# New orders in the attention of a ViT block, and a bias row added to h by GpSimd

## The reference

```
h = tokens(x)                                   # 5 shifted copies, layer norm over 3840 features, @ w (3840 x 192) + b
h = h + attention(layernorm(h))                 # 12 heads of 16, out @ out_w.T + out_b
h = h + experts(layernorm(h))                   # 8 experts, the two largest of a softmax, gelu(x @ w1 + b1) @ w2 + b2
```

## Time and profile before

| | |
|---|---|
| median of 3 runs | 201.43 us (200.71 to 201.55) |
| the profiled execution, its own time | 201.66 us |
| its span, first to last instruction | 199.9 us |
| PE busy | 178.9 us (89%) |
| DVE busy | 142.8 us (71%) |
| ACT busy | 115.4 us (58%) |
| POOL busy | 77.6 us (39%) |
| TensorE on the chain that ended last | 69% of the span |
| granted TensorE clock, mean | 0.983 |

### The profile page before, as it was taken

The page is one execution under the profiler, slowest core; times in us unless marked ns, Lnnn a source line. Parts: engine busy times, 40 slices in busy tenths (PEclk is TensorE's granted clock), DMA queues, the critical chain, the costliest instruction groups (busy, mean ns, idle before and its releaser), DMA issues.

```text
span 199.9 us, 3458 instructions
## 1 busy us (share of the span) xinstructions
PE 178.9 (89%) x1136; PEld 154.3 (77%) x1136; DVE 142.8 (71%) x319; ACT 115.4 (58%) x206; POOL 77.6 (39%) x102
## 2 busy tenths in 40 slices
PE   0599999985798987698999999999999999999994
PEld 0489749954566845577899999989989999989894
DVE  5487994498908638449976976878869869778753
ACT  2485753741221428456569579677596696785540
POOL 7873001125805051187034546266245344462000
PEclk9999999999859999999999999999999999999999
DMA  6999999100010177002700280450630810000002
GB/s 123 223 303 298 260 225 227 29 0 2 0 39 3 31 260 183 3 0 69 208 3 0 65 210 0 135 141 2 183 93 2 239 34 2 0 3 0 0 0 79
DMA packets 14691, 18.38 MB, mean 92 GB/s; under 512 B 2435, under 2 KB 10744, under 8 KB 14678
## 3 DMA queue, kind: packets, MB, share of 16 engines
q1 hardware_dynamic: 14134, 18.19, 34.3%
q10 hardware_dynamic: 544, 0.03, 0.2%
HBM read 17.44 MB, written 0.39 MB: 89 GB/s over the span
## 4 chain that ended last, share of the span: by engine, by line
PE 69%; DVE 11%; issue 6%; DMA 5%; ACT 3%; POOL 2%; SPq 2%; DVEq 0%; POOLq 0%; ACTq 0%
PE ps L371 30%; PE ps L1140 16%; PE ps L1142 7%; DMA early<-in_x 4%; DVE big_r L1215 3%; PE ps L826 2%; PE ps L1002 2%; PE ps L1184 1%; PE ps L1183 1%; DVE merge L1286 1%; PE ps L1182 1%; DVE norm L1393 1%; PE ps L939 1%; PE ps L828 1%; DMA shifted<-shifted 1%
## 5 line engine op out<-in xcount | busy, mean ns | idle before, releaser
L371 PE MATMUL ps<-big_r,wsplit 128*128 128x512 f32 (+1 forms) x255 | 62.8, 383 | 0.0
L1140 PE MATMUL ps<-wsplit,big_r 128*128 128x384 f32 x168 | 49.7, 355 | 0.7 <-DVE big_r L1215 0.7
L751 ACT ACTIVATE early<-ps,b1t 128x512 f32<-128x512 f32 x48 | 32.8, 683 | 29.8 <-PE ps L371 29.8
L1215 DVE TENSOR_TENSOR big_r<-early,big_r 128x512 fp32r<-128x512 f32 x48 | 38.4, 802 | 16.1 <-ACT big_r L333 15.6
L371 PEld LDWEIGHTS ps<-big_r,wsplit 128*128 128x128 f32 x255 | 43.1, 188 | 6.4
L1142 PE MATMUL ps<-wsplit,big_r 128*128 128x192 f32 x168 | 42.1, 250 | 0.0
L1140 PEld LDWEIGHTS ps<-wsplit,big_r 128*128 128x128 f32 x168 | 31.5, 188 | 3.0 <-DVE big_r L1215 0.9
L1142 PEld LDWEIGHTS ps<-wsplit,big_r 128*128 128x128 f32 x168 | 32.0, 190 | 1.3
L333 ACT ACTIVATE big_r<-early 128x512 fp32r<-128x512 f32 x48 | 30.3, 632 | 1.5
L1550 DVE SCALAR_TENSOR_TENSOR merge<-sq,gates,merge 128x192 f32<-128x192 f32 x32 | 26.9, 864 | 0.0
L1574 DVE SCALAR_TENSOR_TENSOR t_a<-ps,gates,merge 128x192 f32<-128x192 f32 x28 | 10.3, 412 | 6.3 <-PE ps L1142 6.3
(11 more groups left out here) (227 smaller groups left out, 290.3 us busy)
## 6 DMA issues: line engine op xcount, KB each, us to landing
stage<-in_L_ffn_w SPq DMA_DIRECT2D x4, 576.0 KB, 6.1
early<-in_L_ffn_w SPq DMA_DIRECT2D x4, 576.0 KB, 5.8
shifted<-in_L_tok_w SPq DMA_DIRECT2D x6, 288.0 KB, 9.6
early<-in_x SPq DMA_DIRECT2D x3, 512.0 KB, 7.0
stage<-in_L_ffn_w SPq DMA_DIRECT2D x4, 384.0 KB, 4.0
stage<-in_L_ffn_w SPq DMA_DIRECT2D x8, 192.0 KB, 4.9
early<-in_L_ffn_w SPq DMA_DIRECT2D x4, 384.0 KB, 3.2
early<-in_L_ffn_w SPq DMA_DIRECT2D x8, 192.0 KB, 3.8
```

The lines of the kernel that those rows point to most:

```text
L371: mm = nc.tensor.matmul(dst, lhs, rhs, start=(first and n == 0), stop=(last and n == 4))
L751: nc.scalar.activation(gf[:, j % NG], ps[:, HPB[j % 4], :], ACT.Gelu, bias=b1t[:, bass.ds(k, 1)]).then_inc(s_gelu, 1)
L1140: nc.tensor.matmul(ps[:, AB[t], 0:2 * D], g_hi[:, j % NG, tok], w2c, start=(f == 0), stop=False)
L1215: return nc.vector.tensor_tensor(o, a, b, op)
```

## The change

It touches four engines' lists.

- GpSimd waits for both low parts of `n1` (`s_nlo` at 2) before it begins the low parts of expert 0.
- GpSimd then adds `const_row` to all of `h` in place (128 x 768 elements), waiting for `s_n` (all of `n1` written, so `h` is no longer read by the norm) and for `s_row`. `constant_rows` and its two TensorE products are gone; `projection` starts the bank itself; `residual` waits for the new semaphore `s_hrow`.
- TensorE makes `values(2)` and `values(3)` right behind `transposed_k(1)`; `repeated_v(0)` and `repeated_v(1)` move behind `near_by_heads(1)`.
- ScalarE copies the values of group 1 before `near_rows(1)`; the four `split_high(1, ...)` of expert 1 are spread over the attention: two behind `values(0)`, one behind `transposed_p(0)`, one behind `exponentials(1)`. None is left behind the gelu table.

```diff
--- before.py
+++ after.py
@@ -236,8 +236,8 @@
         s_ptps, s_pt, s_pv, s_nvp, s_nv, s_pvn, s_ao, s_aodup = (
             sem(n) for n in ("s_ptps", "s_pt", "s_pv", "s_nvp", "s_nv", "s_pvn", "s_ao", "s_aodup"))
 
-        s_vbias, s_row, s_at, s_ahi, s_alo, s_op, s_h2 = (
-            sem(n) for n in ("s_vbias", "s_row", "s_at", "s_ahi", "s_alo", "s_op", "s_h2"))
+        s_vbias, s_row, s_hrow, s_at, s_ahi, s_alo, s_op, s_h2 = (
+            sem(n) for n in ("s_vbias", "s_row", "s_hrow", "s_at", "s_ahi", "s_alo", "s_op", "s_h2"))
 
         s_n2t, s_n2hi, s_n2lo = (sem(n) for n in ("s_n2t", "s_n2hi", "s_n2lo"))
         s_rl, s_rlsb, s_rt, s_gsub, s_gexp, s_gtop, s_gidx, s_gate = (
@@ -550,8 +550,14 @@
                 if g == 0:
                     rstd(0, 0)
             rstd(0, 1)
+            pool.wait_ge(s_nlo, G)
             split_low_w1(pool, 0, 0)
             split_low_w2(pool, 0, 0)
+
+            pool.wait_ge(s_n, TT)
+            pool.wait_ge(s_row, 1)
+            nc.gpsimd.tensor_tensor(h[:, :, :], h[:, :, :], const_row[:, :].unsqueeze(1).broadcast_to([P, TT, D]),
+                                    ALU.add).then_inc(s_hrow, 1)
 
             def near_values(g):
 
@@ -720,26 +726,26 @@
             last_columns_again(0, 1, n1)
             high_parts(1, s_nt, NTB, nt, s_nhi)
             values(0)
+            act.wait_ge(s_emb, G)
+            act.wait_ge(d_stage[1], 16 * STAGE_DMAS)
+            split_high(1, 0)
+            split_high(1, 1)
             near_rows(0)
             transposed_q(1)
             exponentials(0)
+            values(1)
             near_rows(1)
             transposed_p(0)
-            values(1)
+            split_high(1, 2)
             exponentials(1)
+            split_high(1, 3)
             transposed_p(1)
-            act.wait_ge(s_emb, G)
-            act.wait_ge(d_stage[1], 16 * STAGE_DMAS)
-            split_high(1, 0)
             for g in range(G):
 
                 act.wait_ge(s_ao, g + 1)
                 copy(ao[:, 2 * g:2 * g + 2, D:], ao[:, 2 * g:2 * g + 2, P:D]).then_inc(s_aodup, 1)
                 high_parts(g, s_at, ATB, aot, s_ahi)
             nc.scalar.activation(table_in[:], neg_half[:, 0:1], ACT.Gelu)
-            split_high(1, 1)
-            split_high(1, 2)
-            split_high(1, 3)
             for g in range(G):
                 last_columns_again(1, g, n2)
                 high_parts(g, s_n2t, N2B, n2t, s_n2hi)
@@ -1035,12 +1041,6 @@
                                           ptsb[:, b * S:(b + 1) * S], vbd[0:PROWS, b], start=True, stop=True)
                 mm.then_inc(s_pv, 1)
 
-            def constant_rows(g):
-
-                pe.wait_ge(s_pt, g + 1)
-                nc.tensor.matmul(ps[:, OB[g], 0:2 * D], ones_f[0:1, :],
-                                 const_row[0:1, :].unsqueeze(1).broadcast_to([1, 2, D]), start=True, stop=False)
-
             def projection(g):
 
                 pe.wait_ge(s_ahi, g + 1)
@@ -1048,7 +1048,7 @@
                 for n in range(2):
                     tok = slice((2 * g + n) * P, (2 * g + n + 1) * P)
                     mm = triple(ps[:, OB[g], n * D:(n + 1) * D], lambda a: aot[:, a, tok],
-                                wx_(slice(OUT0, OUT0 + D)), True, first=False, last=(n == 1))
+                                wx_(slice(OUT0, OUT0 + D)), True)
                 mm.then_inc(s_op, 1)
 
             pe.wait_ge(s_meansq, 1)
@@ -1089,22 +1089,20 @@
             transposed_q(1)
             near_scores(0)
             transposed_k(1)
+            values(2)
+            values(3)
+            strided_scores(1)
+            near_by_heads(1)
             repeated_v(0)
             repeated_v(1)
-            strided_scores(1)
-            near_by_heads(1)
             transposed_p(0)
-            values(2)
-            values(3)
             near_scores(1)
             strided_values(0)
             repeated_v(2)
             repeated_v(3)
             transposed_p(1)
-            constant_rows(0)
             transposes(0, ao, s_ao, lambda t: t // 2 + 1, ATB, s_at, s_aodup)
             strided_values(1)
-            constant_rows(1)
             projection(0)
             pe.wait_ge(s_vbd, TT)
             transposes(1, ao, s_ao, lambda t: t // 2 + 1, ATB, s_at, s_aodup)
@@ -1498,6 +1496,7 @@
             def residual(g):
 
                 dve.wait_ge(s_op, g + 1)
+                dve.wait_ge(s_hrow, 1)
                 ts = slice(2 * g, 2 * g + 2)
                 tt(h2[:, ts], h[:, ts], ps[:, OB[g], 0:2 * D].rearrange("p (t n) -> p t n", t=2),
                    ALU.add).then_inc(s_h2, 1)
```

## The result

| | before | after |
|---|---|---|
| median of 4 runs | 201.49 us (200.71 to 205.25) | 192.54 us (192.19 to 195.73) |
| ratio, with its 95% interval | | 0.9562 (0.9524 to 0.9601) |
| profiled execution, its own time | 201.66 us | 192.19 us |
| its span | 199.9 us | 190.5 us |
| PE, DVE, ACT, POOL busy | 178.9, 142.8, 115.4, 77.6 us | 170.2, 140.1, 115.6, 80.4 us |

The change makes the kernel faster by 9 us. The ratio leaves out the slowest run of each kernel (205.25 and 195.73 us), which lies over 1.5% above that kernel's fastest.

A forecast was written before the change was run, and what follows sets the result against it. TensorE was taken as the bound, with 69% of the chain, and gains arising between 38 and 82 us: 3.06 + 2.82 + 1.38 - 0.57 + 0.6 = 7.3, less 0.3, so 201.43 - 7.0 = 194.4 us; range 193.2 to 197.4.

The forecast's parts named there:

- values sooner: Second half of the attention: group 1's values made before `repeated_v`, so `outputs(1)` gains 1.38 us more than the maximum.
- Collision of the normalisations: First norm, group 1: with GpSimd waiting for `s_nlo`, VectorE's two normalisations fall from 3.73 to 0.67, gaining 3.06 us.
- Clock: TensorE after the gap at 48.28 to 51.75 us: without the gap the clock stays full, gaining 2.82 us.
- The clock falls all the same: Rival, chance 0.16: TensorE's clock still falls, early or in a remaining shorter gap; price 2.8, giving 197.2 us.
- One of the shorter gaps: Within the clock rival: TensorE's remaining waits at 66.5, 70.0 or 74 us, where the clock might fall; price 2.8.
- Addition: GpSimd before `near_values(0)`: adding 768 columns takes 2.0 us (bounds 1.80 and 2.64), so `outputs(0)` waits 0.2.
- costs nothing either way: `outputs(0)` and `near_values(1)` holding each other cost 0, since ScalarE's duplicate of `ao(0)` waits for `transposed_p(1)` until 64.8.
- Given back: From `outputs(1)` to `projection(1)`: `projection(0)` no longer lies inside the wait for GpSimd, losing 0.57 us.
- Splits: Second norm: ScalarE's splits no longer delay the duplicates of `n2`, gaining 0.6 us; their new places are covered.
- I take 0.3 off for semaphore steps: Deduction of 0.3 us from the summed gain for semaphore steps on the six changed links, leaving 7.0.
- GpSimd as the bound: Rival, chance 0.15: slower addition or blocked denominators put 0.6 to 1.5 us into the chain at 61 to 63 us.
- GpSimd blocking everything: Rival, chance 0.02: GpSimd blocks every VectorE instruction, those from PSUM too, costing 8.4 us and giving 202.8 us.

The follow-up runs named there:

- e9: The change with the addition to `h` moved between `near_values(0)` and `near_values(1)` on GpSimd: 192.6 us.
- e7: The change with the constant rows made by TensorE again and no addition to `h` on GpSimd: 193.52 us.
- e14: The kernel before plus GpSimd's wait for `s_nlo` and the new order of values and `repeated_v`; constant rows and splits as before: 193.83 us.
- e6: The change with the four `split_high(1, ...)` of expert 1 back in their old places on ScalarE: 193.17 us.
- last version: The change with the addition between the near values and GpSimd's power of the gates ahead of expert 1's `w2` low parts, without warm products: 191.62 us.

## Why the forecast was right, and where it failed

The mechanisms were right: collision, clock and late DMA went as forecast. What failed are sizes in the sum. The gain up to the router was put at 7.3 and then 7.0; it was 7.99. The term that failed most is *values sooner*, put at 1.38 by a walk that was too long, and measured at 1.72: 0.34. The first maximum adds 0.16, the stretch behind `outputs(1)` 0.19, and 0.3 was taken off without a row. With all that set right the forecast would be 193.4, still inside the range; what puts the median below it are another 0.9 us, for which the prediction has no term.

- *Collision of the normalisations, 3.06.* Right: 0.67 after, 3.73 without the wait and 3.80 with the gap filled. GpSimd's low parts are where they were put, 50.07 + 1.45 = 51.52 on the clock of before against 51.5.
- *Clock, 2.82.* Right, with its cause: 2.89 with the gap filled and nothing else (2.77 against the second profile of before). "The clock falls all the same" came true in three partial kernels but not in the change. "One of the shorter gaps" fits only one of them: the kernel with the old order of the values, where the fall comes 1.0 us behind a gap of 2.00. With the wait alone (66.5 us) and with the gap filled (68.8) TensorE had no gap over 0.2 us in the 2 us before it. I had not foreseen that the order of the values also guards against that fall; it is worth 1.6 us beside its own 1.74.
- *Values sooner, 1.38.* Right in kind; 1.72 measured. Here lies the step that failed first, the walk along TensorE's list: "`transposed_p(0)` to 60.95, `near_scores(1)` to 61.5" came at 59.66 + 1.45 = 61.11, and the duplicate of `ao(0)`, forecast for 64.8, at 64.33. I added whole durations of groups, but neighbours in the timeline overlap by 0.1 to 0.2 us, so each joint added a little. In the row of `outputs(1)` the sum of it is 0.50.
- *Addition, 2.0.* It took 1.80, the lower bound, the subtraction of the same size. Read from both sizes, 2 x 1.00 - 1.80 = 0.20 of the 1.00 does not grow with the columns (an estimate), and my scaling counted it twice. `outputs(0)` waited 0.24 for it, as forecast (0.2), but that GpSimd's lateness there "costs nothing either way" was wrong: the duplicate of `ao(0)` started 0.04 behind VectorE's held product (61.78 + 1.06 = 62.84), and TensorE waited 0.53 for that product. It cost some 0.18, which the addition between the near values gives back (e9). The edit as a whole was worth 0.21 where I had counted 0 (e7). That it speaks against the engine split of the Trainium skill, "GPSIMD Engine Reference", § 4.1 Engine selection, did little harm here: moving it off the place ahead of `near_values(0)` brought 0.18 in N to R and nothing in the time.
- *Given back, -0.57.* Measured -0.49.
- *Splits, 0.6.* The total of 0.81 is near, but 0.55 of it is the one part that stood ahead of the duplicate of `ao(0)`; the prediction passed over it there and put all 0.6 at the second norm, where 0.26 was due. In the sum the 0.55 is part of the 1.72: with the splits in their old places that term is 1.18 (e14). The walk already had them moved, so its 1.38 held this part without naming it. The 0.26 and the 0.49 given back are not apart either: from `outputs(1)` to the router it takes 8.19 before, 8.22 in e6 and 7.96 in the change, so what is given back at `projection(1)` is regained by the router in any case.
- *"I take 0.3 off for semaphore steps".* Wrong. No row stood behind it; the steps were already in the walk, which was too long and not too short.
- *Rivals.* No reduction or reciprocal was held: the reduction `den` of group 1 started at 63.70, while the addition that GpSimd began at 63.65 ran, and took 0.39 as alone. GpSimd as the bound came about in kind (it stands on the chain up to `outputs(0)`), at 0.18 instead of 0.6 to 1.5. GpSimd blocking everything did not come about; nothing was given back in the experts (117.55 and 117.59).

The whole error: 0.69 in the walk (0.16 at the first maximum, 0.34 to `outputs(1)`, the rest behind it), 0.3 taken off, and 0.9 by which the medians differ more (8.9) than N to R (8.0). The last is no effect that I could tie to an edit. The first stage, whose code is the same, differed by 1.45 us in the two profiled executions; and runs of the kernel before have mean clocks from 0.991 (span 197.1) to 0.949, so some run longer at the lower clock than its profile shows and some less, while the change has none below 0.998. If the stretch behind the first normalisation was as long in every run as in the profiles, the two medians would put its start at about 42.1 before and 41.3 after (an estimate, from 201.43 and 192.54 less the profiled lengths); both lie inside the spread of unchanged kernels, so chance in the first stage could make all of it. It is not shown, and how much each makes is open. The range's lower end, 193.2, allowed for neither.

## What to carry to other kernels

Ask which gap stands ahead of a stretch of lowered clock, and count the clock as part of the price of the wait that made the gap: here one `wait_ge` was worth 5.85 us when it was taken out of the change, about half of it by the clock, and 4.23 us when it was added alone, because the clock then fell elsewhere. When you walk a list with durations from a timeline, calibrate the walk first on a stretch of the old trace, and take nothing off without a row. Compare two executions from a common point of the program, not from their starts, and give the range the spread of the unchanged stages.

## What the runs showed that I had not expected

- *A fall of the clock behind busy TensorE.* In the kernel with the wait alone the clock fell at 66.5 us, with TensorE busy all of the 1.5 us before; in the one with wait and order it was busy 0.73 of 2 and 0.49 of 2 us in two windows and stayed at 1.00. The rule of the Trainium skill ("TensorE: Matmul & The Clock Gate", § HAM oscillation) that idle gaps throttle TensorE is borne out by the gap at 48 us (filled, no fall there), not by this fall nor by the one with the gap filled (68.8 us). The second constant row's products (0.91 to 0.96 us) stand right ahead of both, but they stand in the same place in e14, which kept its clock, and are missing in the kernel of the third late fall. What the three kernels with a late fall have in common is the old order of the values; what in it matters, and whether TensorE's part or ScalarE's, was not tested.
- *Longer transposes at the start, without a sign in the granted clock.* The eight first transposes took 1.09 us in the change's profile and 1.97 in that of the last version, while the granted clock reads 1.00 in both; whether TensorE ran at the lower level there is not shown. The row of the timeline and the window, first of the change, then of the last version:

```profile
11.25 1.09 PE L789 MATMUL ps<-band,norm 128*128 128x128 f32 x8 [0.44 <-DVE norm L306]
```

```profile
10.00:12.00 2.00, 1.56 (x12) 1.00 1.03 340
```

```profile
11.18 1.97 PE L791 MATMUL ps<-band,norm 128*128 128x128 f32 x8 [0.21 <-DVE norm L306]
```

```profile
10.00:12.00 2.00, 1.79 (x9) 1.00 1.05 358
```

- *A cast is held by GpSimd too.* 128 x 32 from uint32 took 2.35 us beside GpSimd's subtraction (0.18 without it), while a reduction with one source of 240 columns took its usual 0.39. By the Trainium skill, "SBUF — State Buffer", § Who interferes with whom, the second of a pair that locks waits; the rows above show it in both directions, VectorE's product at 1.06 for 0.56 and GpSimd's two at 2.00 for 1.69.
